# Writing out all pipelined stages of a 15-stage transformer kernel, without loops, registers and counting steps

## The chip, the cores and the metric

The kernel runs on one core of one Trainium2 chip. Its time is the device time of one execution in microseconds (us). The core has five engines that run side by side, each with its own stream of instructions and its own sequencer: TensorE (PE; its weight loads are shown as PEld), VectorE (DVE), ScalarE (ACT), GpSimd (POOL) and SyncE (SP). They are ordered against each other by semaphores alone: an instruction counts one up when it is done, another one waits until it has a value.

## The reference

Four blocks of cross attention and feed-forward are applied to x, 32 batches of 128 rows by 128 columns, with a context of 32 x 128 x 256. Cut to what matters:

```python
# L0: masked cross attention, 16 heads, with a length mask; then a feed-forward with 8 experts, summed
# L1: de-pooling (a linear recurrence over patches) + projection; then a router keeps 15 of 128 tokens,
#     which go through RoPE attention (16 heads) and a GELU feed-forward
# L2: masked cross attention, 8 heads; then a quantised (BitLinear) feed-forward with a 3-tap convolution
# L3: cross attention of projected queries and keys, 8 heads; then latent attention (16 heads, causal, RoPE)
#     and a mixture of 4 experts with the top one chosen
scores = jnp.einsum('bhqd,bhkd->bhqk', q, k) / np.sqrt(HEAD_DIM)
attn = jax.nn.softmax(jnp.where(mask, scores, -inf), axis=-1)
out = jnp.einsum('bhqk,bhkd->bhqd', attn, v)
```

## The kernel before

x, the context, the queries and the keys stay in on-chip memory throughout. The work is cut into 15 stages, run one after the other with all engines meeting in between (`phase_end`, L776). With their place in the profile, in us: preparation (0 to 92), attention L0 (to 307), ffn0 (to 343), depool (to 434), route (to 489), gather (to 576), attention L1 on four tiles of gathered tokens (to 634), expand (to 700), attention L2 (to 854), bit (to 999), cross (to 1087), attention L3 (to 1250), latent (to 1400), attention L4 (to 1614) and expert (to 1893).

A pipelined stage goes through 32 items (batches). Each engine executes steps; in step t it does its first part for item t, its next part for item t-1, and so on, up to a lag `last` of 3 to 8. `whole_steps` (L46) writes the steps. It writes out the first steps (`first`, 8 where the lag is at most 4 and 12 elsewhere), then makes a loop on the engine (`engine.Fori`) whose body is four steps, for the four slots of the buffers (RING = 4), and then writes out the last `last` steps. So 24 or 20 of the 32 new items enter inside the loop. In the loop the item is a register, so that wait values and some addresses are computed by register instructions. In the written-out steps they are constants. Stage L1 has four items and is written out already, and so are gather and expand. The expert stage has a loop of its own (`loop_groups`, L1470), and there is one more in its GpSimd part.

`hold(engine)` (L146) puts a semaphore step of its own ahead of certain instructions: it counts a semaphore `held_...` that nobody waits for, and it takes over the waits that stand before it. It is used in both loops and written-out steps, on PE, ACT and POOL, and once on DVE (L1375). `Link` (L74) orders instructions of one engine; with `held` it does the same (L87, used by `split_max` on POOL).

In the attention stages PE does in one step: half of the raw scores of item b-2 and half of the scores of item b-4 (`halves`, L546, L557, L565); transpositions and small products (`turns`, L610 to L649); the other halves; then probabilities times values of item b-5 (`weighted`, L669). DVE takes row maxima (L318), masks the turned queries (L325), takes the keys (L332 or L336), and divides by the sums (L348, L354, into o_sb). ACT computes the exponentials in two halves (`exps`, L474), copies (L463, L480) and, in L0 and L2, normalises rows (L455). POOL splits the maxima (L412, L413), copies keys and values (L394, L421), adds o_sb (L427), and in L4 applies the causal mask (L434). The two banks of scores are single: PE can't write the next half before ACT has read the last one.

The waits of a matmul of `weighted`, as an example, in their order: v_ready, pv_ready, nmT_ready, o_scaled, probs_ready, then the hold. In the other stages DVE normalises a row (L266), PE turns it (L788, with a hold) and ACT takes it out (L796).

## Time and profile before

| | us |
|---|---|
| runs shown: median (lowest to highest) | 1903.87 (1903.2 to 1908.92) |
| the profiled execution, its own time | 1903.18 |
| its span, first to last instruction | 1901.5 |
| PE busy | 1450.7 |
| DVE busy | 1149.2 |
| ACT busy | 566.9 |
| POOL busy | 295.2 |

### The profile page before, as it was taken

What the parts mean: (1) busy time and instruction counts of PE and PEld (TensorE: products, weight loads), DVE (VectorE), ACT (ScalarE), POOL (GpSimd) and SP (SyncE); (2) the same over time, 40 slices, a digit from 0 to 9 for tenths busy, and PEclk for the clock granted to TensorE, in tenths of its full rate; (3) what the DMA queues carried; (4) which work ended last, traced back from release to release, by engine and by line L of the source; (5) the groups of instructions that cost most, each with busy time, mean ns of one, the idle gap of its engine ahead of it and who ended that gap; (6) DMA issues with size and microseconds to landing.
All of it is one profiled execution on the core that took longest, in us unless ns stands there. A gap on an engine that the chain in (4) does not pass through costs nothing. (4 is left out here: it accounts for less than half of the span.)

```text
span 1901.5 us, 43998 instructions
## 1 busy us (share of the span) xinstructions
PE 1450.7 (76%) x13766; PEld 945.9 (50%) x13766; DVE 1149.2 (60%) x3639; ACT 566.9 (30%) x1218; POOL 295.2 (16%) x883
## 2 busy tenths in 40 slices
PE   0278787786358548778988987867789998699997
PEld 0267674564334326653445566632247776344443
DVE  1656665899633345657883366667757775454543
ACT  0345553223101115642213344411114443111111
POOL 0012220000301003320001123200015554100000
PEclk9679996675558658988998979955559999799999
DMA  9000000000000000000000000000010000000001
GB/s 288 20 2 2 0 0 1 1 0 1 0 1 1 1 0 3 0 1 1 1 0 1 0 2 0 1 1 1 0 44 3 1 0 2 0 1 0 0 0 45
DMA packets 21991, 20.20 MB, mean 11 GB/s; under 512 B 4655, under 2 KB 17275, under 8 KB 21886
## 3 DMA queue, kind: packets, MB, share of 16 engines
q1 hardware_dynamic: 12400, 14.68, 2.7%
q10 hardware_dynamic: 9486, 4.14, 0.9%
q8 instruction: 63, 1.03, 0.2%
q14 instruction: 42, 0.34, 0.1%
HBM read 16.72 MB, written 2.10 MB: 10 GB/s over the span
## 5 line engine op out<-in xcount | busy, mean ns | idle before, releaser
L318 DVE TENSOR_REDUCE neg_max<-ps 128x8 f32<-128x1024 f32 (+1 forms) x264 | 254.1, 963 | 217.8 <-PE ps L557 208.9
L546 PE MATMUL ps<-qTm,kT 32*128 32x512 f32 (+1 forms) x1056 | 256.9, 559 | 59.2 <-issue 25.5
L557 PE MATMUL ps<-kT,qTm 32*128 32x128 f32 x3200 | 248.3, 292 | 0.2 <-DVE kT L336 0.2
L557 PEld LDWEIGHTS ps<-kT,qTm 32*128 32x128 f32 x3200 | 224.0, 203 | 5.9 <-issue 3.4
L474 ACT ACTIVATE probs<-ps,bias_col 128x512 f32<-128x512 f32 (+1 forms) x192 | 159.3, 830 | 178.8 <-PE ps L565 178.5
L669 PE MATMUL ps<-probs,v_wide 128*32 128x128 f32 x3200 | 121.7, 286 | 41.2 <-DVE o_sb L354 33.9
L546 PEld LDWEIGHTS ps<-qTm,kT 32*128 32x128 f32 x1056 | 88.5, 193 | 123.4 <-issue 121.0
L1639 PE MATMUL ps<-kv_all,ctx_all 128*128 128x512 f32 x256 | 134.9, 609 | 5.2 <-DVE kv_all L1550 5.2
L1616 PE MATMUL ps<-q_all,ctx_all 128*128 128x512 f32 x256 | 132.4, 600 | 0.0
L1550 DVE TENSOR_SCALAR kv_all<-ps,b_col 128x512 f32<-128x512 f32 x64 | 48.0, 750 | 117.2 <-PE ps L1616 117.2
L669 PEld LDWEIGHTS ps<-probs,v_wide 128*32 128x32 f32 x3200 | 86.0, 113 | 61.9 <-issue 59.4
L788 PE MATMUL ps<-ident,row 128*128 128x128 f32 x192 | 71.8, 375 | 56.7 <-DVE row L266 45.6
L1574 ACT ACTIVATE kv_all<-ps,b_col 128x512 f32<-128x512 f32 x64 | 44.0, 687 | 217.0 <-PE ps L1616 217.0
L474 ACT ACTIVATE probs<-ps 128x1024 f32<-128x1024 f32 x72 | 73.8, 1025 | 112.5 <-PE ps L565 112.5
L565 PE MATMUL ps<-nmT,sel_max 32*128 32x128 bf16 x1600 | 97.0, 221 | 0.0
L1264 PE MATMUL ps<-tap_w,xqT 128*128 128x512 f32 x192 | 93.4, 623 | 0.0
L412 POOL CAST nm<-neg_max 128x16 bf16<-128x16 f32 (+1 forms) x132 | 26.8, 203 | 414.8 <-DVE neg_max L318 414.8
L649 PE MATMUL ps<-pv_pick,pv 128*128 128x72 f32 (+1 forms) x528 | 86.0, 288 | 3.7 <-ACT pv L480 2.9
L788 PEld LDWEIGHTS ps<-ident,row 128*128 128x128 f32 x192 | 32.5, 169 | 104.6 <-issue 103.2
L325 DVE TENSOR_TENSOR qTm<-ps,hmask 128x512 f32<-128x512 f32 (+1 forms) x132 | 73.2, 554 | 17.0 <-PE ps L622 14.8
L565 PEld LDWEIGHTS ps<-nmT,sel_max 32*128 32x128 bf16 x1600 | 77.8, 96 | 9.7 <-issue 8.5
L1616 PEld LDWEIGHTS ps<-q_all,ctx_all 128*128 128x128 f32 x256 | 49.3, 193 | 61.8 <-issue 61.8
(352 smaller groups left out, 2900.2 us busy)
## 6 DMA issues: line engine op xcount, KB each, us to landing
ctx_all<-in_ctx SPq DMA_DIRECT2D x1, 4096.0 KB, 30.1
out<-x_all SPq DMA_DIRECT2D x1, 2048.0 KB, 8.7
ctx_all<-in_W1T SPq DMA_DIRECT2D x1, 1024.0 KB, 5.4
probs<-in_conv_wT ACTq DMA_DIRECT2D x1, 768.0 KB
w_l<-in_w ACTq DMA_DIRECT2D x2, 256.0 KB
rope<-in_c_rope ACTq DMA_DIRECT2D x1, 256.0 KB
cls_mask<-in_amask ACTq DMA_DIRECT2D x1, 256.0 KB
probs<-in_b_w1T ACTq DMA_DIRECT2D x1, 256.0 KB
```

Source lines behind the costliest of these rows:

```text
L318: nc.vector.tensor_reduce(neg_max[:, k, H2 * u:H2 * u + H2].rearrange("p (a h) -> p a h", a=2), ps[:, 4 * u:4 * u + 2, 0:N].rearrange("p a ...
L325: nc.vector.tensor_tensor(qTm[:, k, 0:N].rearrange("p (i q) -> p i q", i=per), ps[:, 6, 0:128].unsqueeze(1).broadcast_to([128, per, 128]), ...
L474: nc.scalar.activation(probs[:, k % 2, 2 * N * u:2 * N * (u + 1)].rearrange("p (a n) -> p a n", a=2), ps[:, 2:4, 0:N], ACT.Exp, bias=bias) ...
L546: nc.tensor.matmul(score_bank(g), kT[rows_of(g), k, :], qTm[rows_of(g), k, 0:N], start=not masked_scores, stop=False, skip_group_check=True)
L557: last = nc.tensor.matmul(pair_of(u, g)[:, 128 * i:128 * i + 128], qTm[rows_of(g), k, 128 * i:128 * i + 128], kT[rows_of(g), k, :], start= ...
L565: last = nc.tensor.matmul(score_bank(g)[:, 128 * i:128 * i + 128], sel_max[rows_of(g), i, :], nmT[rows_of(g), k, :], start=False, stop=Tru ...
L649: last = nc.tensor.matmul(ps[:, 7, 256 + W * half:256 + W * half + W], pv[:, k % 2, 128 * half:128 * half + 128], pv_pick[:, 0 if heads == ...
L669: last = nc.tensor.matmul(ps[32 * j:32 * j + 32, 7, 128 * half:128 * half + 128], v_tile(k % 2, heads, 4 * half + j, i), probs[:, k % 2, 1 ...
L788: nc.tensor.transpose(ps[:, k % 2, 0:128], row32[:, k % 2, :], ident[:]).then_inc(sem("turned"), 1)
L1264: last = nc.tensor.matmul(dst, xqT[:, k % 2, tap:tap + 128], tap_w[:, tap, :], start=False, stop=tap == 2)
L1616: nc.tensor.matmul(ps[:, c % 2, :], w_up[:, c, :], xm_T[:, k, :], start=True, stop=True).then_inc(sem("mo_hidden"), 1)
L1639: nc.tensor.matmul(ps[:, 4 + e % 2, :], w_down[:, c, :], hid[:, c % 4, :], start=c % 4 == 0, stop=c % 4 == 3).then_inc(sem("mo_down"), 1)
```

## The change

`whole_steps` writes out every step of every pipelined stage, so that each wait is for a constant and no register is needed. All calls of `hold` are removed, with its definition and the `held` of `Link`; the waits that stood before a hold now stand directly before the engine's instruction. `loop_groups` and GpSimd's loop in the expert stage stay. What is computed, in which order on each engine, and all other semaphores stay as they are.

```diff
 def whole_steps(engine, count, last, step):
-    first = -(-(last + RING) // RING) * RING
-    def plain(t):
+    for t in range(count + last):
         step({lag: (t - lag, (t - lag) % RING) for lag in range(last + 1) if 0 <= t - lag < count})
-    if count < first + RING:
-        for t in range(count + last):
-            plain(t)
-        return
-    for t in range(first):
-        plain(t)
-    with engine.Fori(first // RING, count // RING) as round_:
-        for u in range(RING):
-            step({lag: (round_ * RING + (u - lag), (u - lag) % RING) for lag in range(last + 1)})
-    for t in range(count, count + last):
-        plain(t)
...
         self.engine.wait_ge(self.sem, self.base + self.n)
-        if self.held is not None:
-            self.engine.sem_inc(self.held, 1)
...
-        def hold(engine):
-            engine.sem_inc(sem("held_" + engine_name[engine]), 1)
...
                 act.wait_ge(*after("scores", b * 2 + (2 - u)))
                 done(act, "weighted", b - 2, count)
                 bias = bias_col[:, BIASES.index(L), bass.ts(b, 1)] if L in BIASES else 0.0
-                hold(act)
                 nc.scalar.activation(probs[:, k % 2, 2 * N * u:2 * N * (u + 1)].rearrange("p (a n) -> p a n", a=2),
...
                 for half in (1, 0):
                     pe.wait_ge(*after(ready, b * 2 + (2 - half)))
-                    hold(pe)
                     for i in range(deep):
```

## Rows read from the trace of the kernel before

**Rows 1.** The page's part 1: busy us, share of the span, instructions.

```profile
PE 1450.7 (76%) x13766; PEld 945.9 (50%) x13766; DVE 1149.2 (60%) x3639; ACT 566.9 (30%) x1218; POOL 295.2 (16%) x883
```

**Rows 2.** Stretches of L2, L4, cross, route: length, PE, PEld, DVE, ACT, POOL busy, PEclk, DMA.

```profile
735.00:746.13 11.13, 9.29 (x181) 7.46 (x179) 7.89 (x21) 7.28 (x16) 4.27 (x19) 1.00 0.01 1
1437.30:1454.80 17.50, 17.03 (x323) 13.70 (x324) 12.46 (x26) 8.02 (x12) 9.55 (x21) 1.00 0.01 3
1013.40:1023.20 9.80, 9.80 (x46) 6.21 (x45) 3.50 (x12) 4.01 (x13) 1.61 (x4) 1.00 0.00 1
450.60:482.00 31.40, 19.05 (x61) 13.28 (x60) 31.40 (x206) 13.27 (x41) 0.00 (x0) 0.50 0.00 0
```

**Rows 3.** L412 by stretch: count, durations, first and last start; straight then looped, L0, L2, L3, L4.

```profile
L412 POOL CAST nm<-neg_max x4: 203/203/205, 136.0 to 153.1; 128x16 bf16<-128x16 f32 x4
L412 POOL CAST nm<-neg_max x21: 203/204/205, 158.9 to 274.8; 128x16 bf16<-128x16 f32 x21
L412 POOL CAST nm<-neg_max x4: 202/203/203, 734.5 to 745.6; 128x8 bf16<-128x8 f32 x4
L412 POOL CAST nm<-neg_max x21: 201/202/203, 749.5 to 830.2; 128x8 bf16<-128x8 f32 x21
L412 POOL CAST nm<-neg_max x4: 202/202/203, 1121.3 to 1133.7; 128x8 bf16<-128x8 f32 x4
L412 POOL CAST nm<-neg_max x21: 201/203/204, 1133.7 to 1222.5; 128x8 bf16<-128x8 f32 x21
L412 POOL CAST nm<-neg_max x4: 203/204/204, 1447.6 to 1465.1; 128x16 bf16<-128x16 f32 x4
L412 POOL CAST nm<-neg_max x21: 203/204/206, 1465.1 to 1583.8; 128x16 bf16<-128x16 f32 x21
```

**Rows 4.** The same for L796: straight then looped, bit, latent, depool.

```profile
L796 ACT ACTIVATE xqT<-ps x5: 278/279/280, 884.1 to 899.8; 128x128 f32<-128x128 f32 x5
L796 ACT ACTIVATE xqT<-ps x21: 277/279/280, 904.0 to 987.2; 128x128 f32<-128x128 f32 x21
L796 ACT ACTIVATE rowT<-ps,cols x5: 367/368/368, 1277.2 to 1294.4; 128x128 f32<-128x128 f32 x5
L796 ACT ACTIVATE rowT<-ps,cols x21: 367/367/368, 1298.8 to 1387.4; 128x128 f32<-128x128 f32 x21
L796 ACT ACTIVATE rowT<-ps x4: 271/272/272, 363.8 to 370.6; 128x128 f32<-128x128 f32 x4
L796 ACT ACTIVATE rowT<-ps x21: 271/272/278, 373.1 to 425.8; 128x128 f32<-128x128 f32 x21
```

**Rows 5.** L149, the hold, on PE's sequencer: durations in ns min/median/max.

```profile
L149 PEldq EVENT_SEMAPHORE  x1418: 51/51/13240, 93.6 to 1890.8; - x178
```

**Rows 6.** Timeline in L2's straight part: start, us, engine, line, operation, idle before.

```profile
740.73 0.31 PE L565 MATMUL ps<-nmT,sel_max 32*128 32x128 bf16 x4
740.79 0.29 DVE L354 TENSOR_TENSOR o_sb<-ps,inv_den 128x128 f32<-128x128 f32 x1
741.21 0.69 ACT L474 ACTIVATE probs<-ps,bias_col 128x512 f32<-128x512 f32 x1 [0.38 <-PE ps L565]
741.46 0.64 PE L669 MATMUL ps<-probs,v_wide 128*32 128x128 f32 x16 [0.42 <-DVE o_sb L354]
742.16 0.38 ACT L480 ACTIVATE pv<-ps 128x256 f32<-128x256 f32 x1 [0.26 <-PE ps L669]
```

**Rows 7.** Timeline in the expert stage, where PE waits without a hold.

```profile
1639.98 0.69 ACT L1574 ACTIVATE kv_all<-ps,b_col 128x512 f32<-128x512 f32 x1 [15.15 <-PE ps L1616]
1640.72 0.29 PEld L1639 LDWEIGHTS ps<-kv_all,ctx_all 128*128 128x128 f32 x1 [0.64 <-ACT kv_all L1574]
```

**Rows 8.** Timeline in L0's straight part: PE after an exponential.

```profile
141.84 0.70 PE L546 MATMUL ps<-qTm,kT 32*128 32x512 f32 x2 [0.33 <-ACT probs L474]
```

**Rows 9.** DMA queue q8, packets of code: 140 to 179 us, then 179 to 281 us.

```profile
q8 instruction: 6, 0.10, 1.0%
q8 instruction: 1, 0.02, 0.1%
```

More of the change, by code:

```diff
@@ L74, with __init__ @@
 class Link:
-    def __init__(self, engine, signal, item, per_item, held=None):
-        self.held, self.engine, self.per_item, self.n = held, engine, per_item, 0
+    def __init__(self, engine, signal, item, per_item):
+        self.engine, self.per_item, self.n = engine, per_item, 0
         self.sem, begun = signal
@@ L144, in after @@
             return sem(name), n + begun.get(name, 0)
-        def hold(engine):
-            engine.sem_inc(sem("held_" + engine_name[engine]), 1)
-        engine_name = {}
         def sb(name, shape, dt=F32):
@@ L392, in copy_rows @@
                 done(pool, "first_turned", b - 2, count)
-                hold(pool)
                 nc.gpsimd.tensor_copy(key32[:, k % 2, :], src).then_inc(sem("k_row"), 1)
@@ L398, in copy_rows @@
                     done(pool, "last_turned", b - 4, count)
-                    hold(pool)
                     spots = nm3[:, (k + 2) % RING, :].rearrange("p (g c) -> p g c", g=4)[:, :, 8:11]
@@ L404, in split_max @@
             def split_max(b, k):
-                link = Link(pool, after("nm_link"), b, 1, sem("held_gpsimd"))
+                link = Link(pool, after("nm_link"), b, 1)
                 nm = neg_max[:, k, 0:heads].rearrange("p (g i) -> p g i", g=4)
@@ L410, in split_max @@
                 done(pool, "last_turned", b - 2, count)
-                hold(pool)
                 link(nc.gpsimd.tensor_copy(spots[:, :, :, 0], nm))
@@ L419, in copy_v @@
                 done(pool, "weighted", b - 2, count)
-                hold(pool)
                 nc.gpsimd.tensor_copy(v_blocks(k % 2, heads)[:, :, 0:dh],
@@ L425, in add_o @@
                 pool.wait_ge(*after("o_scaled", b + 1))
-                hold(pool)
                 nc.gpsimd.tensor_tensor(x_all[:, b, :], x_all[:, b, :], o_sb[:, k % 2, :],
@@ L432, in cut @@
                 pool.wait_ge(*after("probs_ready", b * 2 + (2 - u)))
-                hold(pool)
                 nc.gpsimd.affine_select(part, part, [[0, 8], [1, 128]], ALU.is_ge, 0.0, base=0,
@@ L472, in exps @@
                 bias = bias_col[:, BIASES.index(L), bass.ts(b, 1)] if L in BIASES else 0.0
-                hold(act)
                 nc.scalar.activation(probs[:, k % 2, 2 * N * u:2 * N * (u + 1)].rearrange("p (a n) -> p a n", a=2),
@@ L572, in mask_strips @@
                     pe.wait_ge(*after("max_taken", (b - 1) * 2 + 1))
-                hold(pe)
                 for a in range(2):
@@ L584, in mask_whole @@
                     pe.wait_ge(*after("max_taken", (b - 1) * 2 + 2))
-                hold(pe)
                 for a in range(2):
@@ L608, in turns @@
                     done(pe, "oT_ready", b, count)
-                    hold(pe)
                     last = nc.tensor.matmul(ps[:, 6, 384:512], oT[:, k % 2, :], post_w, start=True, stop=True)
@@ L613, in turns @@
                     done(pe, "o_scaled", b, count)
-                    hold(pe)
                     last = nc.tensor.transpose(ps[:, 6, 256:384], o_sb[:, k % 2, :], ident[:])
@@ L619, in turns @@
                     done(pe, "k_row", b, count)
-                    hold(pe)
                     nc.tensor.transpose(ps[:, 6, 0:128], row32[:, k % 2, :], ident[:])
@@ L642, in turns @@
                         done(pe, "nm_split", item(3)[0], count)
-                    hold(pe)
                     last = nc.tensor.transpose(bank_b[7][:, 800:928], nm3[:, slot, :], identb[:])
@@ L646, in turns @@
                     b, k = item(6)
-                    hold(pe)
                     for half in range(2):
@@ L664, in weighted @@
                     pe.wait_ge(*after(ready, b * 2 + (2 - half)))
-                    hold(pe)
                     for i in range(deep):
@@ L786, in stage @@
                 wait_reuse(pe, after("rowT"), b, 2)
-                hold(pe)
                 nc.tensor.transpose(ps[:, k % 2, 0:128], row32[:, k % 2, :], ident[:]).then_inc(sem("turned"), 1)
@@ L1307, in copy_ctx @@
                 wait_reuse(pool, after("cr_ctx_turned"), b, 2)
-                hold(pool)
                 nc.gpsimd.tensor_copy(probs[:, k % 2, 256:512], ctx_all[:, b, :]).then_inc(sem("cr_ctx"), 1)
@@ L1327, in turn_ctx @@
                 wait_reuse(pe, after("cr_ctxT"), b, 2)
-                hold(pe)
                 for c in range(2):
@@ L1373, in query @@
                 yield link.count(nc.vector.bn_stats(st, src[:, 256:320]))
-                hold(dve)
                 yield link.count(nc.vector.bn_aggr(m[:, 0:2], st))
@@ L1439, in turn_latent @@
                 wait_reuse(pe, after("la_latentT"), b, 2)
-                hold(pe)
                 nc.tensor.transpose(ps[0:LATENT, 4 + k % 2, 0:128], o_sb[:, k % 2, 0:LATENT],
@@ L1586, in prepare @@
                 pe.wait_ge(sem("mo_normed"), i * 4 + 4)
-                hold(pe)
                 for j in range(4):
@@ L1599, in prepare @@
                 pe.wait_ge(sem("mo_choice"), i + 1)
-                hold(pe)
                 nc.tensor.transpose(bank_b[3][:, 128:256], nm3[:, 0, :], identb[:]).then_inc(sem("mo_choice_turned"), 1)
@@ L1620, in turn_back @@
                 pe.wait_ge(sem("mo_total"), i + 1)
-                hold(pe)
                 for j in range(4):
@@ L1924, in run @@
         def run(engine, name):
-            engine_name[engine] = name
             begun.clear()
```

## The prediction

> **What bounds the kernel now.** First the page's busy line: no engine is full. TensorE (PE) has 76% of the span, VectorE (DVE) 60%, ScalarE (ACT) 30% [rows 1]. So for most of the time something waits for something, and the question for each stage is whether the waits hang on sequencer steps that the change takes out. Second, the busy time of steady stretches, which sorts the stages. In L2 PE works 9.29 of 11.13 us and DVE 7.89: a chain through several engines sets the step. In L4 PE works 17.03 of 17.50 us (97%), so little can be won. In cross PE is busy for 9.80 of 9.80 us, and in route DVE for 31.40 of 31.40: there the sequencers run ahead of a full engine, and I give these two stages nothing [rows 2].
>
> Third, and this carries the argument, the kernel holds its own comparison. Each pipelined stage runs its first steps and its last ones written out, and only the middle in a loop with registers. The rhythm of a stage can be read as the distance between equal instructions of neighbouring items: once where the pipeline is already full but the code still straight, and once in the loop. GpSimd's L412 runs once a step in the attention stages [rows 3], ACT's L796 once a step in the others [rows 4].
>
> **Part 1: the loops go.** Per stage, looped minus straight rhythm, times the 20 looped distances (24 items less 4; the rows give first and last start):
> - L0: (274.8-158.9)/20 = 5.80, against (153.1-136.0)/3 = 5.70; 0.095 x 20 = 1.9 us.
> - L2: 80.7/20 = 4.035 against 11.1/3 = 3.70; 6.7 us.
> - L3: 88.8/20 = 4.44 against 12.4/3 = 4.13; 6.1 us.
> - L4: 118.7/20 = 5.935 against 17.5/3 = 5.83; 2.0 us [all rows 3].
> - bit: 83.2/20 = 4.16 against 15.7/4 = 3.925; 4.7 us.
> - latent: 88.6/20 = 4.43 against 17.2/4 = 4.30; 2.6 us.
> - depool: 52.7/20 = 2.635 against 6.8/3 = 2.27; 7.4 us [rows 4].
> Sum 31.4 us. The clock is the same on both sides in L0, L2, L3, L4 and bit (full) and in latent (half); in depool it changes several times inside the loop, so that its 7.4 is the softest term. L1 has four items and no loop now; the expert stage keeps its own loop, which the diff leaves; gather, expand and the preparation never had one. For ffn0 I take nothing here.
>
> **Part 2: the extra semaphore steps go.** A hold is an instruction of its own that carries the waits and counts a semaphore nobody reads. On PE's queue one takes at least 51 ns, and there are over a thousand of them [rows 5]. Without it, I expect the first wait in the list to ride on the engine instruction itself and only the others to need a separate step. (The rows show both forms.) In L2, ACT's L474 has a hold: L565 ends at 740.73+0.31 = 741.04, L474 starts at 741.21, 0.17 us later. ACT's L480 waits directly: L669 ends at 741.46+0.64 = 742.10, L480 starts at 742.16, 0.06 us later [rows 6]. So a hold in front of an exponential costs 0.11 us, twice a step. On PE a direct wait costs 0.05 us (L1574 ends at 1639.98+0.69 = 1640.67, L1639 loads at 1640.72) [rows 7]; for each hold that sits on the path there I take the 0.05 us of its own duration. Where several waits queue up the price is higher: o_sb is finished at 740.79+0.29 = 741.08 and L669, which needs five waits and a hold, starts at 741.46, 0.38 us later [rows 6]. Five waits plus a hold are three steps, five waits with one on the matmul are two: a third of it, 0.11 us.
>
> Which of these lie on the path differs by stage. L0's exponentials are the longest, and PE stands idle for 0.33 us until one ends [rows 8]; I take both halves of a step to be so: 2 x 0.11 + 0.05 = 0.27 us, x 32 items = 8.6. In L2 the exponentials and the branch L354 to L669 end close together, so only the branch's gain counts safely: 0.11 + 2 x 0.05 = 0.21, x 32 = 6.7. L3 goes through the same branch and drops two holds more: 0.11 + 3 x 0.05 = 0.26, 8.3 us. L4 drops seven holds a step, but PE is full: 3 x 0.05 = 0.15, 4.8 us. L1, with 12 steps that are nearly all filling and draining, 0.25 each, 3.0. Latent's chain runs through DVE, with one hold there; at PE's price 0.05 x 32 = 1.6. The same in ffn0, where PE's transposition has one: 1.6. Sum 34.6 us. The bounds are wide. The low end is 0, if another branch is as late as the one that is shortened. It isn't below 0: the waits themselves stay, and every form that is left stands in the trace. The high end has every dropped step on the path: 0.11 x 4 on PE and 0.22 on ACT in L0 and L2 (0.66 a step), 0.88 in L3 and 0.99 in L4, x 32 = 102 us. I stay near the low third since PE in L4 and PE and DVE together in L2 are near full.
>
> **Part 3: what it adds.** More code, none of it in the data path. PE's queue of instruction packets shows it: 6 packets of 16 KB in the 39 us of straight code at L0's start, 1 in the 102 us after it [rows 9]. The straight rhythm of 5.70 us is measured while those six arrive, so a fetch costs nothing there, and I price it at zero. If its cover is gone it is a rival, below. No semaphore wait, DMA or buffer is added, and no order of work changes, on any queue.
>
> Total: 31.4 + 34.6 = 66.0 us off the profiled execution's 1903.2, that is 1837.2. The median of the runs shown lies 0.7 us above that execution, so **1838 us**.
>
> **Rivals.**
> Holds hidden (chance 0.17): the loops' part comes, the holds' part doesn't, because in attention DVE's chain from the raw scores over L318 to o_sb sets the step whatever ACT does. For it: DVE is at 71% in L2 and its chain ends next to the exponentials. Against it: three of PE's steps lie inside that very chain. 1903.9 - 31.4 = 1872.
> More than forecast (0.16): waits chained over engines shorten together, and the fill and drain steps, which I counted only once per item, gain too. With the holds' part twice as large: 1903.9 - 31.4 - 69 = 1803.
> Slower (0.05): code fetch. At 6 packets in 39 us, the looped stretches of the four long attention stages (116+81+89+119 = 405 us) need some 62 packets more, those of bit, latent and depool (225 us) up to 35 more, 97 in all on PE alone. It decides if each holds its engine for more than 66/97 = 0.68 us; at 1 us each the time is 1838+97 = 1935. Against it stand the even distances of the straight parts [rows 3, 9]; for it, that in those parts only the first steps of a stage were straight, so that a buffer may have been filled during the stage change.
> The Trainium skill bears on this one: "Runtime: NRT & Kernel Launch", section "Instruction fetch mechanics", says that a long kernel streams its code, that crossing a block is mostly hidden, and that a taken branch out of the buffered pages costs a fetch. By that rule, the trace agrees: fetch adds nothing.
> The change doesn't do what it says (0.02): the compiler still puts the waits in steps of their own and fill time swallows the rest: within 0.3%, 1904.
> The Trainium skill's page "Advanced Engine Details and Errata", section "Sequencer Loop", has other engine instructions read and queued while the sequencer executes a control instruction. If that covered every hold and register step, nothing would move; the 0.1 to 0.33 us between looped and straight rhythm speak against it here.
>
> **How the numbers follow.** Forecast 0.60, hidden holds 0.17, more 0.16, slower 0.05, no effect 0.02. The range runs from 1800 (just past the second case up) to 1882 (past 1872, with depool's soft term gone too); it leaves out the slower case, the unchanged one and the tail of "more", together some 0.15. About 0.3% is what a measurement of this kernel can tell from no change. Faster by over 0.3%: 0.60+0.17+0.16 = 0.93; within: 0.02; slower: 0.05.
>
> **What the changed profile would show.** Part 1 right: L412 and L796 evenly spaced through a stage, nearly no register steps outside the expert stage. Part 2 right: from L565 to L474 0.06 us; L0's step near 5.4, L2's near 3.5, L3's near 3.9, L4's near 5.7. Holds hidden: steps of 5.70, 3.70, 4.13, 5.83 with ACT's or PE's idle time grown. Fetch: gaps of PE with releaser "issue" at regular distances, next to instruction packets. The prediction fails if DVE's chain leaves no room, or if the clock granted to PE falls in a stage that has it in full now.

## The result, and the profile after

| | before | after |
|---|---|---|
| median of the runs, us | 1903.5 | 1814.0 |
| lowest to highest, us | 1900.1 to 1908.9 | 1811.2 to 1817.2 |
| profiled execution, us (its span) | 1903.2 (1901.5) | 1814.5 (1812.7) |
| granted clock, mean share | 0.823 | 0.839 |

The ratio after to before is 0.9528, with a 95% interval from 0.950 to 0.9555. The change takes 89.6 us; the forecast was 66, so the time lies inside the range, 24 us under the forecast and 11 above the rival "more than forecast".

The page's busy line of the changed kernel (busy us, share of the span, instructions) has the instruction counts of [rows 1]. PE is busy for 34.0 us less, DVE for 9.0. Part of PE's is the clock: in ffn0 alone its busy time went from 28.0 to 23.9 us, at a mean granted share of 0.81 in place of 0.59. For PE, the other 56 us are waiting that has gone.

```profile
PE 1416.7 (78%) x13766; PEld 920.7 (51%) x13766; DVE 1140.2 (63%) x3639; ACT 565.5 (31%) x1218; POOL 288.8 (16%) x883
```

The rows that answer [rows 2], of the changed kernel: one stretch of L2, L4, cross and route each (length; PE, weight loads, DVE, ACT and POOL busy; granted clock; DMA share; GB/s).

```profile
735.00:746.13 11.13, 9.95 (x196) 8.13 (x190) 7.93 (x22) 7.59 (x17) 4.99 (x23) 1.00 0.02 4
1400.00:1417.50 17.50, 17.50 (x330) 14.29 (x329) 13.21 (x28) 8.50 (x13) 10.20 (x23) 1.00 0.01 3
960.00:970.00 10.00, 10.00 (x47) 6.32 (x46) 3.65 (x13) 4.29 (x13) 1.61 (x4) 1.00 0.01 2
420.00:450.00 30.00, 17.72 (x60) 11.84 (x59) 30.00 (x197) 12.54 (x40) 0.00 (x0) 0.50 0.01 1
```

In L2 PE does 9.95 us of work in 11.13 where it did 9.29; in L4 it went from 17.03 to 17.50 of 17.50, which is full. Cross and route were full and are what they were. Over the middle of L0, L2, L3, L4 and bit the granted clock is 1.00 in both kernels, and in latent 0.50 in both, so the shorter rhythm there isn't the clock's.

The rhythm, against [rows 3] and [rows 4]: L412 is L386 in the changed kernel, L796 is L755 (count, durations in ns, first and last start). L0, L2, L3, L4, then bit, latent, depool.

```profile
L386 POOL CAST nm<-neg_max x19: 203/204/206, 162.8 to 259.9; 128x16 bf16<-128x16 f32 x19
L386 POOL CAST nm<-neg_max x18: 201/202/203, 731.0 to 790.0; 128x8 bf16<-128x8 f32 x18
L386 POOL CAST nm<-neg_max x20: 202/202/203, 1085.8 to 1158.9; 128x8 bf16<-128x8 f32 x20
L386 POOL CAST nm<-neg_max x21: 203/204/204, 1381.0 to 1495.4; 128x16 bf16<-128x16 f32 x21
L755 ACT ACTIVATE xqT<-ps x19: 277/279/280, 863.1 to 933.3; 128x128 f32<-128x128 f32 x19
L755 ACT ACTIVATE rowT<-ps,cols x19: 367/368/368, 1229.7 to 1305.7; 128x128 f32<-128x128 f32 x19
L755 ACT ACTIVATE rowT<-ps x25: 271/271/278, 340.6 to 396.5; 128x128 f32<-128x128 f32 x25
```

One distance fewer than the count: L0 97.1/18 = 5.39 us, L2 59.0/17 = 3.47, L3 73.1/19 = 3.85, L4 114.4/20 = 5.72; bit 70.2/18 = 3.90, latent 76.0/18 = 4.22, depool 55.9/24 = 2.33. The prediction had named 5.4, 3.5, 3.9 and 5.7.

The branch of L2 that answers [rows 6]: L565, L354, L474, L669, L480 have become L533, L331, L443, L629, L449 (start, us, engine, line, operation, idle before).

```profile
740.37 0.31 PE L533 MATMUL ps<-nmT,sel_max 32*128 32x128 bf16 x4
740.49 0.29 DVE L331 TENSOR_TENSOR o_sb<-ps,inv_den 128x128 f32<-128x128 f32 x1
740.74 0.69 ACT L443 ACTIVATE probs<-ps,bias_col 128x512 f32<-128x512 f32 x1 [0.22 <-PE ps L533]
741.03 0.65 PE L629 MATMUL ps<-probs,v_wide 128*32 128x128 f32 x16 [0.36 <-DVE o_sb L331]
741.74 0.38 ACT L449 ACTIVATE pv<-ps 128x256 f32<-128x256 f32 x1 [0.31 <-PE ps L629]
```

L533 ends at 740.37+0.31 = 740.68 and L443 starts at 740.74: 0.06 us, where it was 0.17. From the end of L331 (740.78) to L629 it is 0.25 us, where it was 0.38.

The code's packets, the queue of [rows 9], from 140 to 281 us of the changed kernel: 21, where there were 6+1 = 7. Over the whole execution the page has 113 packets on this queue (q8) for 63 before; a second queue of code, q14, has 60 smaller ones for 42. In that stretch L0 keeps its 5.39 us.

```profile
q8 instruction: 21, 0.34, 1.0%
```

### The profile page after: what moved, and what is told of

Its sections match the earlier page's. It is cut to its first block and busy times, and to the rows that moved or that the text cites. A ratio compares the mean times of both kernels' runs of the same rounds, so it can differ in the third digit from the quotient of the medians.

```text
span 1812.7 us, 37968 instructions
## 1 busy us (share of the span) xinstructions
PE 1416.7 (78%) x13766; PEld 920.7 (51%) x13766; DVE 1140.2 (63%) x3639; ACT 565.5 (31%) x1218; POOL 288.8 (16%) x883
## 5 line engine op out<-in xcount | busy, mean ns | idle before, releaser
L514 PE MATMUL ps<-qTm,kT 32*128 32x512 f32 (+1 forms) x1056 | 251.9, 551 | 25.8 <-DVE neg_max L295 14.6
L443 ACT ACTIVATE probs<-ps,bias_col 128x512 f32<-128x512 f32 (+1 forms) x192 | 159.3, 830 | 131.0 <-PE ps L533 131.0
L629 PE MATMUL ps<-probs,v_wide 128*32 128x128 f32 x3200 | 118.2, 281 | 33.4 <-DVE o_sb L331 27.3
L747 PE MATMUL ps<-ident,row 128*128 128x128 f32 x192 | 69.3, 362 | 54.8 <-DVE row L243 44.5
L629 PEld LDWEIGHTS ps<-probs,v_wide 128*32 128x32 f32 x3200 | 84.9, 111 | 51.6 <-issue 47.9
L443 ACT ACTIVATE probs<-ps 128x1024 f32<-128x1024 f32 x72 | 73.8, 1025 | 115.8 <-PE ps L533 115.8
L533 PE MATMUL ps<-nmT,sel_max 32*128 32x128 bf16 x1600 | 93.6, 218 | 0.0
L386 POOL CAST nm<-neg_max 128x16 bf16<-128x16 f32 (+1 forms) x132 | 26.8, 203 | 384.7 <-DVE neg_max L295 384.7
L302 DVE TENSOR_TENSOR qTm<-ps,hmask 128x512 f32<-128x512 f32 (+1 forms) x132 | 73.2, 554 | 15.5 <-PE ps L585 13.5
L533 PEld LDWEIGHTS ps<-nmT,sel_max 32*128 32x128 bf16 x1600 | 73.2, 95 | 10.2 <-issue 8.8
```

Source lines behind the costliest of these rows:

```text
L302: nc.vector.tensor_tensor(qTm[:, k, 0:N].rearrange("p (i q) -> p i q", i=per), ps[:, 6, 0:128].unsqueeze(1).broadcast_to([128, per, 128]), ...
L443: nc.scalar.activation(probs[:, k % 2, 2 * N * u:2 * N * (u + 1)].rearrange("p (a n) -> p a n", a=2), ps[:, 2:4, 0:N], ACT.Exp, bias=bias) ...
L514: nc.tensor.matmul(score_bank(g), kT[rows_of(g), k, :], qTm[rows_of(g), k, 0:N], start=not masked_scores, stop=False, skip_group_check=True)
L533: last = nc.tensor.matmul(score_bank(g)[:, 128 * i:128 * i + 128], sel_max[rows_of(g), i, :], nmT[rows_of(g), k, :], start=False, stop=Tru ...
L629: last = nc.tensor.matmul(ps[32 * j:32 * j + 32, 7, 128 * half:128 * half + 128], v_tile(k % 2, heads, 4 * half + j, i), probs[:, k % 2, 1 ...
L747: nc.tensor.transpose(ps[:, k % 2, 0:128], row32[:, k % 2, :], ident[:]).then_inc(sem("turned"), 1)
```

## The experiments

Where the 89.6 us came from is told by the length of each stage: from the last engine's drain at the end of one stage to the last one at the end of the next, in the trace. Gather, expand, route and cross, which stay within 0.6 us, are left out of the table. "Loops only" is e1; us.

| stage | before | loops only (e1) | after |
|---|---|---|---|
| L0 | 215.2 | 214.8 | 201.3 |
| ffn0 | 36.6 | 30.5 | 30.6 |
| depool | 90.7 | 83.6 | 83.6 |
| L1 | 58.4 | 58.3 | 58.7 |
| L2 | 153.6 | 145.3 | 132.6 |
| bit | 145.8 | 139.4 | 139.8 |
| L3 | 163.2 | 150.2 | 140.6 |
| latent | 150.1 | 147.2 | 145.1 |
| L4 | 214.2 | 214.3 | 206.5 |
| expert | 278.2 | 277.4 | 278.9 |

And the two sizes into which an attention stage falls: the time from the first to the seventh L412 (or L386), which is how long it takes to fill, and the mean distance of 20 in its middle.

| | fill L0 / L2 / L3 / L4 | distance L0 / L2 / L3 / L4 |
|---|---|---|
| before | 36.5 / 26.2 / 27.0 / 36.5 | 5.794 / 4.035 / 4.441 / 5.934 |
| e1 | 36.6 / 24.3 / 25.7 / 38.4 | 5.693 / 3.721 / 4.018 / 5.851 |
| e2 | 35.9 / 25.7 / 26.4 / 36.2 | 5.641 / 3.640 / 3.869 / 5.732 |
| e3 | 31.1 / 24.2 / 23.2 / 34.9 | 5.460 / 3.582 / 4.003 / 5.839 |
| e4 | 32.2 / 22.0 / 21.1 / 35.3 | 5.393 / 3.467 / 3.860 / 5.715 |
| after | 30.7 / 21.8 / 22.8 / 34.8 | 5.393 / 3.467 / 3.861 / 5.720 |

Each row is one profile, and some parts of a stage differ between kernels that are the same there. L0 is the same, instruction for instruction, in the changed kernel, e7, e8 and e10: the stage takes 200.2 to 203.0 us, its filling 30.7, 31.9, 33.0 and 31.9, and the time from the last L386 to the stage's end, called its tail here, 22.1, 20.3, 18.8 and 22.6. In the same four, filling takes 19.9 to 21.8 us in L2, 20.9 to 22.8 in L3 and 34.7 to 35.4 in L4, L1 takes 56.0 to 58.7, and cross 87.0 to 89.8. The distances agree within 0.02 us. So a distance is a firm witness, and a filling or a stage is one only beyond 2 or 3 us.

### e1: the loops out, the holds kept

The changed kernel with every hold that the change dropped put back.

```diff
+        def hold(engine):
+            engine.sem_inc(sem("held_" + engine_name[engine]), 1)
...
+                hold(act)
                 nc.scalar.activation(probs[:, k % 2, ...],
...
+                hold(pe)
```

> Every pipelined stage written out, all holds kept: part 1 of the sum alone. Theory (two additive parts): 32.8 us off the 1903.5 of before (31.4 of the sum and 1.4 for ffn0), so 1871 us, within 1866 to 1876, with attention steps of 5.70 (L0), 3.70 (L2), 4.13 (L3), 5.83 (L4). Rival A (the 24 us beyond the forecast belong to the loops: a loop also costs something at its entry, its exit and in the granted clock of the stages around it): 1850 or less. Rival B (holds and loops cost the same path, so that either alone gives nearly all): below 1835.

Measured: 1859.4 us (1856.0 to 1864.6), ratio 0.9768 (0.9744 to 0.9792). The two parts of the change are thus worth 1903.1-1859.4 = 43.7 us and 1859.4-1814.0 = 45.4 us. L412 is L398 here; L0, L2, L3, L4:

```profile
L398 POOL CAST nm<-neg_max x22: 202/203/205, 165.1 to 284.6; 128x16 bf16<-128x16 f32 x22
L398 POOL CAST nm<-neg_max x21: 200/201/202, 741.3 to 815.7; 128x8 bf16<-128x8 f32 x21
L398 POOL CAST nm<-neg_max x18: 200/201/203, 1123.2 to 1191.5; 128x8 bf16<-128x8 f32 x18
L398 POOL CAST nm<-neg_max x18: 202/203/204, 1451.7 to 1551.0; 128x16 bf16<-128x16 f32 x18
```

That is 119.5/21 = 5.69, 74.4/20 = 3.72, 68.3/17 = 4.02 and 99.3/17 = 5.84 us. The straight stretches at the head of each stage of the kernel before had given 5.70, 3.70, 4.13 and 5.83 [rows 3]. Three of four agree within 0.02 us; L3's head had not yet settled. The same loops without the holds weren't tried.

### e2, e3, e4: the holds of one engine each

The changed kernel with one `hold(act)` ahead of each exponential of attention (e2), with the holds on PE in attention (e3), with those on GpSimd in attention (e4).

> The changed kernel with one hold back, that before the exponentials on ScalarE. Theory: the hold is on L0's path twice a step (step 5.39 to 5.61 us), in L2 and L3 about once (3.47 to 3.58, 3.86 to 3.97), in L4 not (5.72 stays): about 7+4+4 us, 1829 us, within 1822 to 1836. Rival (VectorE's chain from the raw scores to o_sb sets the step and hides ScalarE): steps unchanged, 1814 to 1818 us.

> The changed kernel with TensorE's nine holds of the attention stages back. Theory: 0.05 us a step in L0 (5.44), 0.21 in L2 (3.68), 0.26 in L3 (4.12), 0.15 in L4 (5.87), with the steps of filling some 25 us in all: 1839 us, within 1831 to 1846. Rival (TensorE's sequencer runs ahead of the array, so its steps are hidden and ScalarE's hold was the whole gain): steps as in the changed kernel, 1814 to 1820 us.

> The changed kernel with GpSimd's holds of the attention stages back. Theory: the full steps don't hang on GpSimd, which waits 2 us a step for the row maxima, so 5.39, 3.47, 3.86 stay; while a stage fills, the maxima are on the path once per item, 0.26 us for some five items in five stages: 1814 to 1821 us. Rival (the split of the maxima is late for the turning on TensorE in every step): 0.1 us or more a step, 1828 us or more.

Measured: e2 1844.1 us (1843.8 to 1845.8), 30.1 more than after; e3 1831.3 (1826.2 to 1833.4), 17.3 more; e4 1812.2 (1811.1 to 1813.8), no different. Together 30.1+17.3 = 47.4, against 45.4 for all holds at once: the prices add up, and two engines carry them. Per item the distances say where. The hold at the exponential costs 0.248 us in L0, 0.173 in L2, 0.008 in L3 and 0.012 in L4; those on PE 0.067, 0.115, 0.142 and 0.119. e2 shows the cause in two lines of L2 (L543 and L453 stand for L533 and L443):

```profile
745.20 0.31 PE L543 MATMUL ps<-nmT,sel_max 32*128 32x128 bf16 x4
745.68 0.69 ACT L453 ACTIVATE probs<-ps,bias_col 128x512 f32<-128x512 f32 x1 [0.43 <-PE ps L543]
```

745.68-745.51 = 0.17 us again, where the changed kernel has 0.06. For e2 the forecast was 1829: I had priced its steady cost alone. It also adds to the filling of L0 and L2 (35.9 for 30.7 us, 25.7 for 21.8) and L3 (26.4 for 22.8), where it costs nothing per item. In all three e2 lies above what the four kernels without holds show. The other two forecasts: e3 had 1839 and a price of 0.05 in L0, 0.21 in L2, 0.26 in L3 and 0.15 in L4, too much in all but L0; e4 had 1814 to 1821 us and the distances unchanged, which they are.

### e5: a clock raised before the first item

Five unread 128x512 matmuls (four in L3, not in L2 as the expectation has it) on PE at the start of L0, L2, L3 and L4.

```diff
+        def warmed(phase, n):
+            t = phase["tensor"]
+            def tensor(pe):
+                for _ in range(n):
+                    nc.tensor.matmul(ps[:, 5, :], ident[:], ident[:].unsqueeze(1).broadcast_to([128, 4, 128]),
+                                     start=True, stop=True)
+                t(pe)
+            return dict(phase, tensor=tensor)
```

> The changed kernel plus five matmuls of 128x512 whose result nobody reads (four in L2), issued by TensorE at the start of each of the stages L0, L2, L3 and L4, while VectorE computes the first items' moments. Theory (part of what the first items of a stage gained hangs on the granted clock, which stands at 1.2 GHz when a stage starts and rises only when TensorE has work): the clock is granted earlier, the first to the seventh item take 3 to 6 us less in each of the four stages: 1790 to 1803 us. Rival (the first items hang on the chain of waits from engine to engine, and the clock is a by-product): 1811 to 1818 us.

Measured: 1803.6 us (1802.3 to 1809.8), ratio 0.9473 (0.9446 to 0.9499): 10.4 less than after, at the edge of the first expectation. The total hides a split. L0 is 5.2 us shorter and L4 3.5, L2 1.1 and L3 not at all (+0.4). The expectation wanted 3 to 6 us less between the first and the seventh item in each of the four; L4 alone has that (30.2 for 34.8), L0 has 1.4 less (29.3 for 30.7), L2 and L3 none. In L0 the way to the first L386 is 0.5 us shorter, and the tail 3.2 (18.9 for 22.1). That tail is 18.8 to 22.6 us in kernels without the unread matmuls, so only 1.9 of L0's 5.2 us can be put down to its start. Stretches at the starts of L0 and L2, after, then e5:

```profile
91.00:125.00 34.00, 23.09 (x338) 19.71 (x338) 21.96 (x39) 12.58 (x22) 6.52 (x28) 0.72 0.01 1
673.00:700.00 27.00, 18.16 (x202) 13.68 (x203) 14.88 (x38) 11.74 (x23) 6.55 (x29) 0.56 0.01 2
```
```profile
91.00:125.00 34.00, 27.23 (x383) 19.93 (x383) 22.28 (x41) 13.29 (x24) 7.97 (x34) 0.91 0.01 1
667.00:694.00 27.00, 24.04 (x232) 16.20 (x233) 14.95 (x38) 12.15 (x25) 7.41 (x33) 0.69 0.00 1
```

The granted clock rose in both, from 0.72 to 0.91 and from 0.56 to 0.69. But in L2's start DVE does the same 14.9 us of work in the same 27 (x38 both times): there PE wasn't what the first items waited for. In L0's start it was, for a time, as a shorter stretch of the changed kernel shows, PE busy throughout at 1.2 GHz (0.50):

```profile
104.00:110.00 6.00, 6.00 (x62) 5.25 (x61) 4.31 (x5) 1.94 (x3) 1.11 (x6) 0.50 0.00 0
```

### e6: the late wait issued first

In the trace the first matmul's weight load carries the first wait that was asked for (v_ready in `weighted`), and the others are steps of their own ahead of it, two waits to a step. The waits on the latest event were asked for last. Here they are asked for first.

```diff
+                if s_item is not None:
+                    b, k = s_item
+                    if u == 0:
+                        done(pe, "probs_ready", b - 1, count, 2)
+                    else:
+                        pe.wait_ge(*after("probs_ready", b * 2 + 1))
...
             def weighted(b, k):
+                done(pe, "o_scaled", b - 1, count)
                 done(pe, "v_ready", b, count)
                 done(pe, "pv_ready", b - 1, count)
                 done(pe, "nmT_ready", b + 2, count)
-                done(pe, "o_scaled", b - 1, count)
```

> The changed kernel with the order of two waits on TensorE turned round: ahead of the halves' matmuls the wait for the exponentials, and ahead of the weighted sum the wait for the scaled rows, are issued first, and the others last, so that the steps on their own come while the engine would have waited anyway. Theory (what each step still costs is a wait issued on its own between two matmuls): 0.06 to 0.2 us per item of L0, L2 and L3, 1792 to 1806 us. Rival (the order doesn't matter, since the waits that come early are passed in the matmuls' shadow): 1811 to 1817 us.

Measured: 1794.8 us (1791.2 to 1799.7), ratio 0.9413 (0.939 to 0.9436): 19.2 less than after. The distances fall to 5.211, 3.266, 3.659 and 5.691 us, by 0.18, 0.20, 0.20 and, in the full stage L4, 0.03; and the filling doesn't change in a consistent way. L2 in e6, where L629 is L632:

```profile
739.39 0.29 DVE L331 TENSOR_TENSOR o_sb<-ps,inv_den 128x128 f32<-128x128 f32 x1
739.74 0.64 PE L632 MATMUL ps<-probs,v_wide 128*32 128x128 f32 x16 [0.25 <-DVE o_sb L331]
```

739.74-739.68 = 0.06 us from the rows to the matmul, in place of 0.25. In the changed kernel's trace two steps of 51 ns stand in that gap on PE's sequencer, starting at 740.82 and 740.93; the weights follow at 741.00. With the order turned the weight load carries the wait for o_scaled itself, at 739.74, and no step stands between 739.3 and it: they are passed before. The edit has two places, and they weren't tried apart. In L2 and L3 the gap from the rows to the matmul shrinks by 0.20 us, as much as the distance does.

### e7: the expert stage written out as well

```diff
-            with engine.Fori(0, GROUPS // 2 - 1) as pair:
-                for u in range(2):
-                    body(pair * 2 + (u + 1), (u + 1) % 2)
+            for i in range(1, GROUPS - 1):
+                body(i, i % 2)
```

> The changed kernel with the last loops written out too: the loop over pairs of groups on each engine of the expert stage and GpSimd's loop over its stores. Theory (TensorE idles only 5.8 us of this stage's 278, so the registers' work lies under matmuls): 0 to 3 us less, 1811 to 1815 us. Rival (a loop costs here what it costs in the other stages, 0.2 us or more per item): 8 us less or more, at most 1806 us.

Measured: 1814.1 us (1811.6 to 1815.9), no different from 1814.0; the stage takes 277.7 us for 278.9. Under a full engine a loop costs nothing that shows, as in cross and route, which lost loops and holds and stayed as they were (87.4 and 87.0 us, 54.7 and 54.8). L4 isn't such a case: in e1 its stage is as long as before (214.2, 214.3), but its distance is 0.08 us shorter.

### e8 and e10: why ffn0 gained 6 us

ffn0's loops gave 6.1 us where I had taken nothing. Its mean granted clock had gone from 0.59 to 0.81, so my theory was the clock. e8 puts the loops back in ffn0 alone (with its hold on PE, in the looped steps); e10 is e8 with one unread 128x128 matmul per item.

```diff
-            steps(pe, B, [(1, turn_rows(pe)), (2, multiply)])
+            looped_steps(pe, B, [(1, turn_rows(pe, True)), (2, multiply)])
```
```diff
                 nc.tensor.transpose(ps[:, k % 2, 0:128], row32[:, k % 2, :], ident[:]).then_inc(sem("turned"), 1)
+                if held:
+                    nc.tensor.matmul(ps[:, 5, 0:128], ident[:], ident[:], start=True, stop=True)
```

> The changed kernel with the loops of the stage ffn0 alone put back as they were, with their semaphore step on TensorE. Theory (the 6 us that this stage gained are the clock's: with the loops' pauses TensorE isn't granted 2.4 GHz there): the stage takes about 36 us again, nearly all of it at 1.2 GHz: 1818 to 1822 us. Rival (the loops cost the engines' own time alone, the clock stays as in the straight stage): at most 1.5 us more, 1813 to 1816 us.

> The changed kernel with the loops of ffn0 back (e8, where the stage took 36.6 us at a granted share of 0.55) plus one unread 128x128 matmul on TensorE per item of that stage. Theory (the looped stage is long because TensorE has too little work per item for 2.4 GHz): the added work raises the granted share above 0.7, and the stage gets shorter though it does more: 31 to 34 us, the kernel 1814 to 1818. Rival (the loop's own time makes the stage long, or this much work isn't enough for the clock): 36.6 us or more, since the matmul is added to a busy engine: 1819 to 1824.

Measured: e8 1819.7 us (1816.0 to 1821.2), ffn0 36.6 us long at a clock of 0.55; e10 1820.6 (1820.0 to 1821.9), ffn0 37.7 us long at 0.86. e8 alone looks like a proof of the clock; e10 has the clock and not the gain. The rows of the stage settle it. The changed kernel, first the clock of two stretches, then L755 in them:

```profile
293.00:304.00 11.00, 5.92 (x24) 5.12 (x25) 7.79 (x34) 3.67 (x10) 0.00 (x0) 0.50 0.00 0
306.00:322.00 16.00, 15.50 (x63) 9.03 (x63) 15.24 (x63) 5.83 (x21) 0.00 (x0) 1.00 0.00 1
```
```profile
L755 ACT ACTIVATE rowT<-ps x8: 277/278/278, 298.4 to 303.3; 128x128 f32<-128x128 f32 x8
L755 ACT ACTIVATE rowT<-ps x21: 277/278/278, 306.3 to 321.7; 128x128 f32<-128x128 f32 x21
```

e8, then e10, in the loop (the clock of the stretch, then the same instruction, L777 and L779):

```profile
317.00:329.00 12.00, 11.34 (x36) 8.01 (x35) 9.84 (x37) 3.05 (x11) 0.00 (x0) 0.50 0.00 1
L777 ACT ACTIVATE rowT<-ps x11: 277/277/278, 317.6 to 327.5; 128x128 f32<-128x128 f32 x11
```
```profile
307.00:320.00 13.00, 9.59 (x66) 7.49 (x65) 10.34 (x39) 3.58 (x13) 0.00 (x0) 1.00 0.00 1
L779 ACT ACTIVATE rowT<-ps x13: 277/278/278, 307.0 to 319.0; 128x128 f32<-128x128 f32 x13
```

Straight code has 4.9/7 = 0.70 us at 1.2 GHz and 15.4/20 = 0.77 at 2.4; the loop has 9.9/10 = 0.99 at 1.2 and 12.0/12 = 1.00 at 2.4 (with the added matmul). (The eight at 1.2 GHz are the stage's first items and uneven, 0.64 to 0.77 us apart once two are through.) The clock moves neither. The loop costs about 0.23 us per item by itself; its hold has no part in it, since e1, straight with the hold, has 30.5 us for the stage and the changed kernel 30.6. The higher clock of the straight stage comes with the denser work. The trace of the kernel before has it too (L796 in ffn0; the first row takes in the loop's first items, the second is the loop):

```profile
L796 ACT ACTIVATE rowT<-ps x10: 277/277/278, 312.3 to 319.1; 128x128 f32<-128x128 f32 x10
L796 ACT ACTIVATE rowT<-ps x22: 277/278/278, 320.0 to 341.5; 128x128 f32<-128x128 f32 x22
```

6.8/9 = 0.76 against 21.5/21 = 1.02, a difference of 0.27 us, x 20 = 5.4 us.

### e9 and e12: is the filling the clock's?

e2's hold lengthens L0 by 213.5-201.3 = 12.2 us, of which 32 x 0.248 = 7.9 are its steady price. e9 and e12 ask whether the rest is the clock. e9 is e2 with five unread matmuls at L0's start, e12 is e9 with more of them in the idle time ahead of the first six waits for exponentials.

```diff
+                    if L == "L0" and isinstance(b, int) and b < 3:
+                        for _ in range(3):
+                            nc.tensor.matmul(ps[:, 4 * u, 0:128], ident[:], ident[:], start=True, stop=True)
```

> The kernel with ScalarE's step ahead of the exponentials back (e2) plus five unread matmuls of 128x512 on TensorE at the start of L0 alone. With the step and without the matmuls L0 took 213.5 us, without both 201.3, with the matmuls alone 196.1. Theory (of the 12.2 us that the step costs in L0, about 0.25 us per item over the whole stage is its own time, some 7 us, and the rest is the clock, which with the step falls back to 1.2 GHz among the first items): with the matmuls the clock holds, and L0 takes 202 to 206 us, the kernel 1833 to 1838. Rival (the rest is the chain of waits of the first items, whatever the clock): the matmuls bring no more than the 5 us that they brought without the step, L0 at 208 or above, 1839 or above.

> The kernel with ScalarE's step ahead of the exponentials (e2) and the five unread matmuls at the start of L0 (e9), plus three unread 128x128 matmuls on TensorE ahead of each of its first six waits for the exponentials in L0, where in e9 it idled 0.7 to 1.9 us each time and was at 1.2 GHz again from 104 to 125 us. Theory (what L0's first items lose with the step is mostly the clock's): 2.4 GHz is kept through the first items, and L0 takes 202 to 206 us in place of 213.9, the kernel 1833 to 1838 us. Rival (the first items hang on the chain of waits from engine to engine, at either clock): the clock is kept but L0 takes 208 us or more, the kernel 1839 or above. If the clock isn't kept, the run tells nothing.

Measured: e9 1847.3 us (1833.7 to 1849.1; three of its four at 1845.9 and above), e12 1835.1 (1834.6 to 1835.9). From 110 to 125 us, e9, e12, and the changed kernel:

```profile
110.00:125.00 15.00, 11.01 (x133) 9.32 (x130) 6.69 (x9) 6.55 (x9) 2.06 (x10) 0.50 0.01 1
```
```profile
110.00:125.00 15.00, 12.75 (x217) 11.31 (x215) 8.88 (x13) 8.77 (x13) 2.18 (x11) 1.00 0.01 2
```
```profile
110.00:125.00 15.00, 10.77 (x235) 9.13 (x231) 10.37 (x14) 8.60 (x13) 2.79 (x14) 1.00 0.01 2
```

In e9 the clock fell back to 1.2 GHz (0.50), so that its profile tells nothing of the question; L0 took 213.9. In e12 it stayed at 2.4 GHz, and L0 took 207.9 us. The kernel's time meets the first expectation (1833 to 1838), but the stage, on which the question bears, lies between 206 and 208, between the two. About half of the step from e9 to e12 (11.4 us between the profiled executions) falls outside L0, 2.4 of it in L1 and 1.7 in L2, where nothing differs between the two, so the kernel's time is the worse witness here. The fairer pair is e12 with e5: both at the full clock almost from L0's start, with and without the hold: 207.9-196.1 = 11.8 us, against 12.2 for the pair without unread matmuls. Filling takes 32.6 against 29.3, 3.3 us more, where it was 5.2. So by the stage's length the clock accounts for 0.4 us of the 12.2, by the filling for 1.9. Both are within what L0 varies by in kernels where it is the same (2.8 us the stage, 2.3 the filling), and 2.0 of the 11.8 us lie in the tails (20.9 for 18.9). The extra matmuls that e12 has and e5 hasn't take some time themselves, too. So the clock's share isn't shown to be anything, and its size stays open; that it is most of the rest, as the theory had it, isn't borne out. Of the 3.3 us at full clock, 6 x 0.25 = 1.5 are the steady price, and 1.8 come on top, again less than filling varies by.

### e11: the better order and the raised clock together

e6 with the matmuls of e5 at L0 and L4 alone.

> The changed kernel with the order of waits of e6 (19 us less) and the unread matmuls of e5 at the start of L0 and L4 alone, where they brought 5.2 and 3.5 us; in L2 and L3 they brought nothing. Theory (the one acts on the step per item, the other on the clock among the first items, so they add up): 1785 to 1789 us. Rival (with the new order the first items' clock is granted as late as before and the warm clock is lost again after them, or both use the same idle time): 1791 to 1796 us.

Measured: 1785.9 us (1782.9 to 1790.3), ratio 0.9373 (0.9349 to 0.9397). L0 goes from 197.4 to 192.8 and L4 from 204.7 to 201.3 against e6, most of it in the filling (32.3 to 28.5 and 34.6 to 29.5). It is the best of the kernels here, 28 us under the changed one.

## Why the prediction was right, and by how much it missed

**Direction and mechanism** were right: straight code and waits that ride on the instruction shorten the rhythm in every stage that has room. The four named distances came true within 0.05 us, and so did L2's 0.06 us from the matmul to the exponential. For L3's 3.9 that was luck: the straight rhythm was put 0.11 us too high and the holds' price 0.10 too high, and the two cancel. The changed kernel has nearly no register steps left (87 arithmetic ones on PE's sequencer for 905). The loops' time isn't spread evenly: in L2's loop before, distances of 3.91, 3.96, 3.83 and 4.41 us come round, 3.70 when straight, so one item of four bears about half of it. Once in a round each engine also branches back, which takes 215 ns on PE and 45 to 56 on the others; whether the long distance comes from it isn't shown.

```profile
L59 PEldq COMPARE_BRANCH  x53: 76/215/236, 181.2 to 1582.9; - x53
L59 POOLq COMPARE_BRANCH  x28: 40/45/50, 178.0 to 1580.6; - x28
```

**Part 1, 31.4 us forecast, 43.7 measured.** Depool 7.1 (7.4), latent 2.9 (2.6), bit 6.4 (4.7) and L2 8.3 (6.7) were close. Three terms were mis-sized:
- ffn0, "I take nothing here": 6.1 us. This is the plain mistake, a term at nothing without a reason. The rule of the other stages applied to its own rows gives 5.4.
- L3, 6.1 forecast, 13.0 measured. The straight distance of 4.13 us came from three distances at the head of the stage, which hadn't settled; e1 has 4.02, and (4.44-4.02) x 20 = 8.5. The other 4.5 us lie in filling and draining, 1.3 of them in filling and 2.9 in the tail (16.7 for 19.6).
- L0 and L4, 1.9 and 2.0 forecast, 0.4 and none measured. The distances fell as forecast (0.10 and 0.08 us); in L4 filling took 1.9 us more (38.4 for 36.5), which gives it back, and in L0 the tail took 1.6 more (22.2 for 20.6), within what that tail varies by.

**Part 2, 34.6 us forecast, 45.4 measured.** Per item, e1 minus after: L0 0.300 us (0.27 forecast), L2 0.254 (0.21), L3 0.157 (0.26), L4 0.131 (0.15), latent 4.286-4.220 = 0.066 (0.05). Times 32 these are 9.6+8.1+5.0+4.2+2.1 = 29.0 us, where these five terms had 8.6+6.7+8.3+4.8+1.6 = 30.0.

That the sums meet is partly luck, since their make-up doesn't. The failed terms are the 0.05 us for each of PE's further holds and the exponential left out of L2. From the rows o_sb to the matmul of `weighted` it is 0.38 us before and 0.25 after in L2 [rows 6], and 0.38 and 0.26 in L3, here before, then after:

```profile
1181.10 0.29 DVE L354 TENSOR_TENSOR o_sb<-ps,inv_den 128x128 f32<-128x128 f32 x1
1181.77 0.65 PE L669 MATMUL ps<-probs,v_wide 128*32 128x128 f32 x16 [0.59 <-DVE o_sb L354]
```
```profile
1103.51 0.29 DVE L331 TENSOR_TENSOR o_sb<-ps,inv_den 128x128 f32<-128x128 f32 x1
1104.06 0.64 PE L629 MATMUL ps<-probs,v_wide 128*32 128x128 f32 x16 [0.46 <-DVE o_sb L331]
```

So the branch gives its 0.11 or 0.12 us in both. All of PE's holds together cost 0.115 in L2, 0.142 in L3 and 0.119 in L4 (e3), hardly more than that branch alone: the 2 or 3 x 0.05 us for the others are nearly all missing. This split is inferred, as no run has one of PE's holds without the rest. In L2 the exponential, which I had left out as hidden, costs 0.173 (e2) and makes up for it.

The holds were also miscounted: per item PE drops 7 in L0 and L2, 9 in L3 and 11 in L4 (L149 stands 226, 227, 290 and 352 times in these stages), where the high end and the term of L4 had 4, 6 and 7. With the right counts the high end is (7+7+9+11) x 0.11 + 4 x 0.22 = 4.6 us, x 32 = 148, not 102; the forecast itself doesn't use it. ffn0 (1.6) gave nothing, and L1 (3.0) nothing that can be told from its variation of 2.7 us (58.3 and 58.7).

What I left out is the time of filling and draining: over L0, L2, L3 and L4 the stages lost 13.5+12.7+9.6+7.8 = 43.6 us, the steady prices are 26.9 of these, and 16.7 remain. Of them 9.8 lie between the first and the seventh item: filling lost 5.9+2.5+2.9+3.6 = 14.9, and six distances account for 5.1. "Counted only once per item" was the weak step, and the rival "more than forecast" had named it; what it had put at 34 us more was 11. During filling a hold costs more than in the steady rhythm: ScalarE's in L0 5.2/6 = 0.87 us per item in place of 0.25 (e2 against after), 3.3/6 = 0.55 with the clock at 2.4 GHz in both (e12 against e5). Against the slowest filling without holds, 33.0 us, e2's is still 2.9/6 = 0.48; the 0.55 rests on a single pair. That several hops of an item then lie behind one another with no other item's work beside them is the likely reason, argued and not shown.

**Part 3, 0 forecast, 0 measured.** 113 code packets for 63, 21 for 7 in a stretch of L0 that kept an even 5.39 us. The rival "slower" had asked for some 97 packets more and 0.68 us each; 50 came on that queue, and cost nothing that shows. That is also what the page "Runtime: NRT & Kernel Launch" of the Trainium skill, section "Instruction fetch mechanics", would have, and the trace agrees. Nor was PE slow in the loops for want of code: [rows 9] has one packet in 102 us of loop.

**Holds hidden** (1872) is ruled out by e1, which is the change without the holds' part: 1859.4 against 1814.0. The page "Advanced Engine Details and Errata" of the Trainium skill, section "Sequencer Loop", has other instructions queued while the sequencer runs a control instruction; the trace agrees where an engine is full (route, cross, the expert stage in e7) and not where it waits (0.17 against 0.06 us in e2). L4, where PE read 97% busy, still paid 0.13 us per item.

## What to carry to other kernels

A stage's rhythm can be read twice in one trace, in its straight head and in its loop; do it for every stage, also the short ones, and take the head only once it has settled. Sequencer steps were free under an engine that was quite full (cross, route, the expert stage), but not under one at 97% (L4); on a hop of the chain that sets the step they cost more than their own time, and more while a pipeline fills than while it runs. Most steps off that chain cost nothing, so count the hops and not the steps. Read how much a stage varies between kernels that are the same in it before a difference of a few us is given a cause. Ask for the wait that ends last first, so that it rides on the instruction and the others are passed while the engine waits: that brought 19 us here, on top of the 90, for a few moved lines.

## What the runs showed of the hardware

- A higher granted clock beside a shorter stage needn't be its cause. ffn0 has the same distance at 1.2 and at 2.4 GHz (0.70 and 0.77 us straight, 0.99 and 1.00 looped). e8, which changed both at once, had looked like the opposite.
- Work that nobody reads can shorten a kernel: five 128x512 matmuls at a stage's start brought 10.4 us in all (e5). L4 is 3.5 us shorter in e5 and 3.4 in e11 against e6. Up to its seventh item L0 gains 4.4 us in e11 against e6, and 1.9 in e5, which is within what its filling varies by. L2 and L3 gain nothing clear.
- An engine at 97% by its busy time isn't full. In L4 PE worked 17.03 of 17.50 us before, and dropping holds still took 0.13 us off each item.
- A step on a sequencer costs more than its duration: two steps of 51 ns put 0.19 us between the rows and the matmul (0.25 against 0.06), since they start 0.11 us apart.
